# Pairs of score bursts, rows transposed in 32x32 blocks by VectorE, and a reordered hand-over from attention to experts

## The chip, the core and the metric

The kernel runs on one core of one Trainium2 chip. The metric is the device time of one execution in microseconds. Comparisons take the median over runs of both kernels on the same chip.

## What is computed

A gated cross-attention block followed by a gated mixture of experts, all in float32. `x` is 2048 x 256, the context 1601 x 256, there are 16 heads of 64, 8 experts of hidden size 512, and each row goes to its top 2 experts. The mask of the inputs keeps only rows at the end of the context: the kernel tests for that and then works on the last 401 context rows alone (a slower general branch exists and isn't taken).

```python
x = x + tanh(g_xattn) * xattn(layernorm(x), ctx, mask, Wq, Wk, Wv, Wo)
#   scores = q k^T / 8, masked, softmax over the context, times v, times Wo
x = x + tanh(g_ffn) * ffn(layernorm(x), Wg, W1, W2, W3)
#   gate_out = x Wg^T ; top 2 ; softmax of the two
#   per expert e: y = (silu(x W1[e]^T) * (x W2[e]^T)) W3[e]^T ; out += y * weight
```

## The kernel before

**Attention.** Heads go in pairs, rows in four groups of 512 (four tiles of 128). A *duo* is one tile of 128 rows for both heads of a pair; four duos (one group of rows, one pair of heads) are a *chunk*. There are 32 chunks and 128 duos. Every engine runs through the same list of steps n; each engine's `step_of(n)` says what it does in step n, and semaphores alone tie the engines together.

- TensorE (PE): step n has `scores(n)` (L1284): four products with 64 rows of weights, two heads beside one another in the array's halves, into two of the four banks `ps_s`. It is followed by one other piece: `queries` (L1227, `wq_sb`) where n % 4 is 1, `out_projection` (L1321, `wo_sb`) where it is 2, and the two halves of `probs_v` (L1311, the product with v, 64 columns of weights, two heads beside one another) where it is 3 and 0. `scores(d)` waits until VectorE has read duo d-2.
- VectorE (DVE): in step n the reciprocals of the sums of duo n-1 (`inverses`, L1029), scaling, mask and maximum of duo n (`mask_and_max`, L1040, PSUM to `probs`), and the 32x32 block transposes of duo n-2 (`transpose_blocks`, L1052) into `blocksT`.
- ScalarE (ACT): the exponentials of duo n (`exps`, L672), and copies out of PSUM.
- GpSimd (POOL): the division, i.e. the product of duo n-1 with its reciprocals (`scale`, L552).
- `regroup` (L331): when the four duos of chunk c are in `blocksT`, 16 DMAs per chunk (12 from SyncE's queue, 4 from ScalarE's) move the blocks to their partitions in `probsT`. `probs_v(c, 0)` waits for all of them, in step 4c + 11.
- Beside this, after each group of rows is finished, its routing runs in stages s (`routing(r, s)`, from step 47 + 32r on): norms, logits, the top two, positions. In stages 22 to 25 GpSimd scatters the rows of the group into `x_regrouped` in DRAM, sorted by expert: two indirect DMAs (L543) a stage, eight a group. The fourth group's routing runs beside the first expert tiles (`BESIDE`).

**Hand-over.** SyncE (SP) loads expert 0 (three DMAs of 512 KB, L277) between the regrouping of chunks 29 and 30. After the last regrouping has landed it loads expert 1, waits for the table of tiles (`sched_ready`, made by VectorE from step 133 on in pieces) and for the scatters of three groups, loads eight row tiles, and then the other experts.

**Experts.** 36 tiles of 128 rows go through: for tile s PE does `first_hidden(s+1)` (L1491), the transposes of `gated` (L1512), `second_hidden(s+1)` (L1491), `transpose_x` of tile s+2 (L1486: two transposes, copied out by ScalarE at L788) and `project_down(s)` (L1519). VectorE does `gate(s+1)` (L1172) and `weigh(s)`, GpSimd adds the rows to the output with an indirect DMA (L604). A row tile is one DMA of 128 rows of 258 words (`load_tile`, L384).

Of the kernel before, what the change touches and what calls it, by code (L numbers as in the profile page):

```python
# [13 lines left out]
P = 128  # L14
# [47 lines left out]
LAST_STAGE = 25  # L62

BESIDE = ((0, 1, 2, 3), (4, 5, 6, 7), (8, 9, 10), (12, 13, 14), (15, 16), (17, 18, 19, 20, 21), (22,), (23,), (24,), (25,))
# [3 lines left out]
K_STEPS = {0: 2, 6: 3, 7: 4, 8: 5, 10: 6, 12: 7}  # L68
XN_STEP = 20
# [9 lines left out]
def build(nc, x, ctxT, mask, g_xattn, g_ffn, Wq, Wk, Wv, Wo, WgT, W1T, W2T, W3T, out):  # L79
    with ExitStack() as ctx:  # L80
# [105 lines left out]
        with ExitStack() as ffn:  # L186

            w_sb = sb("w_sb", [P, NE, EW], F32, ffn)
            xgT = sb("xgT", [P, 2, KT, P], F32, ffn)
            silu = sb("silu", [P, FH], F32, ffn)  # L190
            to_blocks = sb("to_blocks", [P, 272], F32, ffn)
            xg = sb("xg", [P, RING, XW], F32, ffn)
# [58 lines left out]
        xgT_ps, xgT_ready = sem("xgT_ps"), sem("xgT_ready")  # L251
# [34 lines left out]

        def settled(eng):
# [19 lines left out]
            eng.wait_ge(inv_ready, PRE - 1)  # L307
            eng.wait_ge(scaled, PRE - 1)
            eng.wait_ge(blocks_ready, PRE - 2)
# [30 lines left out]
        def _(sp):  # L340
# [38 lines left out]
            def load_tile(i, k):  # L379
                s = RING * i + k  # L380
                if not first(s, RING):
                    sp.wait_ge(y_ready, s - RING + 2)
                row = table(sp, 0, s, NOWHERE)
                sp.dma_start(xg[:, k % RING, :], x_regrouped[bass.ds(row, P), :]).then_inc(xg_in[k % RING], 16)  # L384

            with sp.If(last_block_only(sp)):
                sp.wait_ge(pads_set, 2)
                for c in range(CHUNKS):
# [18 lines left out]
                for k in range(RING):  # L407
                    load_tile(0, k)
# [3 lines left out]
                load_expert(sp, 3)  # L412
# [48 lines left out]
            for s in range(FULL, NG):  # L461
                sp.wait_ge(xg_in[s % RING], 16 * (s // RING + 1))
# [5 lines left out]
        def _(pool):  # L468
# [33 lines left out]
            def routing(r, s):  # L502
# [37 lines left out]
                if 22 <= s < 22 + GT:  # L540
                    t = s - 22
                    for c in range(2):
# [4 lines left out]
            def scale(d):  # L547

                pool.wait_ge(inv_ready, d + 1)
# [5 lines left out]
            def step_of(n):  # L555
# [8 lines left out]
                if 1 <= n <= DUOS:  # L564
                    scale(n - 1)
# [59 lines left out]
        def _(act):  # L625
# [64 lines left out]
            def step_of(n):  # L690
# [20 lines left out]
                if n % 4 in (2, 3) and 0 <= (n - 6) // 4 < CHUNKS:  # L711

                    c = (n - 6) // 4
                    if n == 6:
# [4 lines left out]
                    for g in (0, 1) if n % 4 == 2 else (2, 3):  # L719
# [66 lines left out]
            def copy_xgT(s, buf):  # L786
                act.wait_ge(xgT_ps, s + 1)
                act.copy(xgT[:, buf, :, :], ps_t[1][:, 0:KT * P].rearrange("p (k n) -> p k n", k=KT))\  # L788
                   .then_inc(xgT_ready, 1)

# [12 lines left out]
            def ffn_tile(i, k):  # L803
# [4 lines left out]
                if not (isinstance(s, int) and s + 2 >= NG):  # L808
                    copy_xgT(s + 2, k % 2)

            act.sem_inc(gatedT_ready, 1)
            copy_xgT(0, 0)
            silu_of(0)
            copy_xgT(1, 1)
# [14 lines left out]
        def _(dve):  # L829
# [87 lines left out]
            def routing(r, s):  # L917
# [17 lines left out]
                if s in (6, 7):  # L935
# [8 lines left out]
                    for t in (2 * s - 12, 2 * s - 11):  # L944
                        dve.tensor_scalar(rows[:, 0, t, 0:D], xs[:, bass.ds(GT * r + t, 1), :].squeeze(1),
# [80 lines left out]
            def inverses(d):  # L1026
                b = 2 * d % RING_P
                dve.wait_ge(probs_ready, 2 * d + 2)
                dve.reciprocal(inv_sum[:, b:b + 2], sum_exp[:, b:b + 2]).then_inc(inv_ready, 1)  # L1029

            def mask_and_max(d):
# [3 lines left out]
                for u in (2 * d, 2 * d + 1):  # L1035
# [4 lines left out]
                    dve.tensor_tensor_reduce(probs[:, b, 0:LASTK], ps_s[u % 4][:, 0:LASTK], biases[:, tile, :],  # L1040
# [25 lines left out]
            def step_of(n):  # L1066
# [12 lines left out]
                if 1 <= n <= DUOS:  # L1079
# [514 lines left out]
```

## Time and profile before

| | |
|---|---|
| three runs, us | 657.89, 657.48, 655.51 (median 657.48) |
| the profiled execution, us | 657.01 |
| its span, first to last instruction | 655.3 us |
| PE busy | 622.2 us, 95% |
| DVE, POOL, ACT busy | 389.9, 308.2, 286.9 us |
| PE busy from 100 to 200 us | 100.00 of 100.00 us |
| PE busy from 394 to 430 us (hand-over) | 27.18 of 36.00 us |
| PE busy from 470 to 560 us (experts) | 90.00 of 90.00 us |
| granted TensorE clock, 400 to 403, 403 to 406, 406 to 409, 412 to 415, 415 to 418 us | 1.00, 0.53, 0.50, 0.76, 1.00 of 2.4 GHz |

The span is cut into three stretches: attention to about 396 us (the last scores), a hand-over to 428.7 us (the first product with an expert's weights), and the experts. 1.7 us of the execution lie outside the span.

### The profile page before, as it was taken

The numbers are of one execution on the slowest core, as the hardware profiler recorded it, in microseconds if no ns is written. First come the engines' busy times: TensorE is split into PE (matmuls) and PEld (weight loads), VectorE is DVE, ScalarE is ACT, GpSimd is POOL, SyncE is SP. The second block draws the span as 40 slices with busy tenths as digits, with TensorE's granted clock in tenths as the row PEclk, the third lists the DMA queues.
The fourth block names the chain that finished last, engine by engine and source line by source line (L and its number), as shares of the span: only waits on it lengthen the run. The fifth ranks groups of instructions, "written<-read, shape, count | busy, mean of one in ns | idle before, by whom it ended". The sixth has DMA issues, their size and how long they took to land.

```text
span 655.3 us, 10748 instructions
## 1 busy us (share of the span) xinstructions
PE 622.2 (95%) x2958; PEld 344.4 (53%) x2959; DVE 389.9 (59%) x1187; ACT 286.9 (44%) x744; POOL 308.2 (47%) x270
## 2 busy tenths in 40 slices
PE   4899999999999999999999997889999999999994
PEld 2444454545455554555544554346666666666653
DVE  3578968888988769978879977243252122221211
ACT  2765566565555545555546552023322222222221
POOL 3643645555564686564786545302463222222221
PEclk9999999999999999999999998899999999999999
DMA  8844675767667578566587769989455322233311
GB/s 320 291 106 106 135 161 124 167 147 164 152 135 185 133 189 184 136 159 162 144 202 147 174 161 239 257 280 355 74 144 124 48 44 47 41 48 48 48 21 22
DMA packets 93420, 95.37 MB, mean 146 GB/s; under 512 B 11312, under 2 KB 86960, under 8 KB 93360
## 3 DMA queue, kind: packets, MB, share of 16 engines
q1 hardware_dynamic: 70800, 71.64, 42.1%
q10 hardware_dynamic: 15840, 14.07, 9.5%
q0 software_dynamic: 6720, 8.95, 8.4%
q8 instruction: 27, 0.44, 0.3%
q14 instruction: 33, 0.27, 0.2%
HBM read 27.72 MB, written 12.36 MB: 61 GB/s over the span
## 4 chain that ended last, share of the span: by engine, by line
PE 76%; POOL 6%; DMA 5%; DVE 5%; issue 4%; ACT 3%; ACTq 1%; SPq 0%; POOLq 0%; DVEq 0%
PE ps_s L1491 17%; PE ps_s L1284 13%; PE ps_o L1311 13%; PE ps_o L1519 8%; PE ps_a L1227 7%; PE ps_a L1321 7%; POOL probs L552 3%; POOL x_regrouped L543 2%; DMA out_dram<-yg,ids 2%; PE ps_t L1512 2%; DVE blocksT L1052 2%; PE ps_o L1297 2%; DVE probs L1040 2%; DMA probsT<-blocksT 1%; PE ps_t L1486 1%
## 5 line engine op out<-in xcount | busy, mean ns | idle before, releaser
L552 POOL TENSOR_TENSOR probs<-probs,inv_sum 128x802 f32<-128x802 f32 x128 | 195.0, 1525 | 155.1 <-DVE inv_sum L1029 154.3
L672 ACT ACTIVATE probs<-probs,neg_max 128x401 f32<-128x401 f32 x256 | 159.3, 624 | 144.3 <-DVE neg_max L1040 144.3
L1040 DVE CUSTOM_DVE_ANT_0 probs<-ps_s,biases 128x401 f32<-128x401 f32 x256 | 136.9, 573 | 57.2 <-PE ps_s L1284 56.0
L1491 PE MATMUL ps_s<-w_sb,xgT 128*128 x296 | 139.5, 594 | 1.4 <-ACT xgT L788 1.4
L1052 DVE STREAM_TRANSPOSE blocksT<-probs 128x832 f32<-128x832 f32 x128 | 133.3, 1041 | 9.3 <-POOL probs L552 9.3
L604 POOL DMA_INDIRECT out_dram<-yg,ids x36 | 56.1, 1558 | 161.1 <-DVE yg L1184 142.9
L1311 PE MATMUL ps_o<-probsT,v_sb 128*64 128x512 f32 x512 | 125.8, 615 | 4.2 <-DMA probsT<-blocksT 4.2
L1284 PEld LDWEIGHTS ps_s<-kT,qT 64*128 64x128 f32 x1024 | 82.3, 186 | 78.0 <-DVE neg_max L1040 38.8
L1284 PE MATMUL ps_s<-kT,qT 64*128 64x201 f32 (+1 forms) x1024 | 121.2, 355 | 0.7 <-ACT qT L636 0.7
L1172 DVE TENSOR_TENSOR gated<-ps_s,silu 128x512 f32<-128x512 f32 x37 | 25.6, 692 | 118.5 <-PE ps_s L1491 113.1
L801 ACT COPY gatedT<-ps_t 128x512 f32<-128x512 f32 x36 | 21.1, 586 | 120.5 <-PE ps_t L1512 120.5
L1491 PEld LDWEIGHTS ps_s<-w_sb,xgT 128*128 128x128 f32 x296 | 53.0, 190 | 39.6 <-issue 38.0
L1519 PE MATMUL ps_o<-w_sb,gatedT 128*128 x288 | 68.1, 379 | 0.0
L1321 PE MATMUL ps_a<-wo_sb,oT 128*128 128x256 f32 x240 | 60.7, 397 | 4.0 <-ACT qT L636 3.7
L1227 PE MATMUL ps_a<-xnT,wq_sb 128*128 128x512 f32 x128 | 63.2, 616 | 0.8 <-ACT xnT L640 0.8
L1311 PEld LDWEIGHTS ps_o<-probsT,v_sb 128*64 128x64 f32 x512 | 31.8, 138 | 59.9 <-issue 54.6
L1519 PEld LDWEIGHTS ps_o<-w_sb,gatedT 128*128 128x128 f32 x288 | 51.9, 190 | 5.6
L1321 PEld LDWEIGHTS ps_a<-wo_sb,oT 128*128 128x128 f32 x240 | 43.7, 192 | 16.4 <-ACT qT L636 10.1
L672 ACT ACTIVATION_READ_ACCUMULATOR probs<-probs,neg_max 128x1 f32 x256 | 47.8, 187 | 0.0
L1184 DVE TENSOR_SCALAR yg<-ps_o,xg 128x256 f32<-128x256 f32 x36 | 17.4, 484 | 42.1 <-PE ps_o L1519 42.1
L543 POOL DMA_INDIRECT x_regrouped<-rows,place x32 | 31.7, 990 | 9.2 <-issue 8.3
L1227 PEld LDWEIGHTS ps_a<-xnT,wq_sb 128*128 128x128 f32 x128 | 21.8, 189 | 24.3 <-issue 24.3
(143 smaller groups left out, 418.0 us busy)
## 6 DMA issues: line engine op xcount, KB each, us to landing
probsT<-blocksT SPq DMA_DIRECT2D x285, 96.0 KB, 3.2
probsT<-blocksT SPq DMA_DIRECT2D x95, 128.0 KB, 2.6
probsT<-blocksT ACTq DMA_DIRECT2D x99, 96.0 KB, 3.2
xg<-x_regrouped SPq DMA_DIRECT2D x39, 129.0 KB, 2.1
probsT<-blocksT ACTq DMA_DIRECT2D x33, 128.0 KB, 2.7
w_sb<-W1T_dram SPq DMA_DIRECT2D x8, 512.0 KB, 7.8
w_sb<-W2T_dram SPq DMA_DIRECT2D x8, 512.0 KB, 8.5
w_sb<-W3T_dram SPq DMA_DIRECT2D x8, 512.0 KB, 9.4
```

Of the source, the lines that this page charges most:

```text
L543: pool.indirect_dma_start(out=x_regrouped, out_offset=bass.IndirectOffsetOnAxis(ap=place[:, c, t:t + 1], axis=0), in_=rows[:, c, t, :], in ...
L552: pool.tensor_tensor(duo, duo, inv_sum[:, u:u + 2].unsqueeze(2).to_broadcast([P, 2, LASTK]), ALU.mult)\
L604: pool.indirect_dma_start(out=out, out_offset=bass.IndirectOffsetOnAxis(ap=ids[:, k % RING:k % RING + 1], axis=0), in_=yg[:, k % 2, :], in ...
L672: act.activation(probs[:, b, 0:LASTK], probs[:, b, 0:LASTK], ACT.Exp, bias=neg_max[:, b:b + 1], scale=-1.0, accum_out=sum_exp[:, b:b + 1]) ...
L1040: dve.tensor_tensor_reduce(probs[:, b, 0:LASTK], ps_s[u % 4][:, 0:LASTK], biases[:, tile, :], HD ** -0.5, 3e38, ALU.add, ALU.min, neg_max[ ...
L1052: dve.transpose(blocksT[:, c % 2, :, :, t * 32:(t + 1) * 32].rearrange("p c u n -> p u c n"), probs[:, u:u + 2, :].rearrange("p u (c n) -> ...
L1227: mm = pe.matmul(ps_a[:, :], wq_sb[:, k, p * P:(p + 1) * P], xnT[:, k, i * GQ:(i + 1) * GQ], start=(k == 0), stop=(k == KT - 1))
L1284: mm = pe.matmul(ps_s[(2 * d + odd) % 4][:, k0:k1], qT[h0:h0 + HD, c % 2, t * P:(t + 1) * P], kT[h0:h0 + HD, c % HP, k0:k1], start=True, s ...
L1311: mm = pe.matmul(ps_o[odd * HD:(odd + 1) * HD, :], v_sb[:, s, 2 * (c % HP) + odd, :], probsT[:, c % 2, s, :, odd, :], start=(s == 0), stop ...
L1321: mm = pe.matmul(wo_bank(g, half)[:, n * D:(n + 1) * D], oT[:, c % 4, t * P:(t + 1) * P], wo_sb[:, c % HP, :], start=(c == 2 * g), stop=(c ...
L1491: mm = pe.matmul(bank[:, :], xgT[:, buf, k, :], w_sb[:, bass.ds(expert, 1), (n * KT + k) * FH:(n * KT + k + 1) * FH].squeeze(1), start=(k ...
L1519: mm = pe.matmul(ps_o[:, 0:D], gatedT[:, k, :], w_sb[:, bass.ds(expert, 1), 2 * KT * FH + k * D:2 * KT * FH + (k + 1) * D].squeeze(1), sta ...
```

## The change

1. **Bursts.** From duo 24 (`BURST`) on, PE does the scores of two duos in a row, in even steps, into six banks (the four `ps_s` and the two `ps_t`); a duo now waits for VectorE to have read the duo three before it.
2. **Two duos per reciprocal; everything behind it a step later.** VectorE inverts the sums of two duos in one instruction in even steps. `scale` is at step d + 2, `transpose_blocks` at step d + 3, ScalarE's share of the regrouping a step later. `probs_v` stays in its steps.
3. **Scatters.** One indirect DMA a stage over eight stages instead of two over four, for the first two groups; the third keeps two a stage. `BESIDE` keeps two a tile for the fourth.
4. **Block transposes of rows.** The row tile is loaded by five DMAs instead of one: four bring 64 of the 256 columns each, to 32 partitions, as pieces of 64 words (256 bytes); the fifth brings the two words of weight and row number. VectorE then makes `xgT` in one block transpose of 128 x 256, three tiles ahead. PE's `transpose_x` and ScalarE's copy are gone. The rows are stored with their columns in another order, and `WgT` is laid out to match.
5. **Hand-over.** SP loads no expert and stores no output rows while the last chunks are regrouped. After them: expert 0, the waits for table and scatters, tiles 0 and 1, the sign that expert 0 is there, expert 1, tile 2, the store of the third group, expert 2, and then for e = 3 to 7 tile e, expert e and the sign for expert e-1. VectorE makes the table of tiles in one go in step 133.

```diff
+BURST = 24
...
+        def scores_bank(u):
+
+            return ps_s[u % 4] if u < 2 * BURST else (ps_s + ps_t)[(u - 2 * BURST) % 6]
...
-                sp.dma_start(xg[:, k % RING, :], x_regrouped[bass.ds(row, P), :]).then_inc(xg_in[k % RING], 16)
+                tile = x_regrouped[bass.ds(row, P), :]
+                for q in range(4):
+
+                    sp.dma_start(xg_blocks[32 * q:32 * q + 32, k % RING, :, :],
+                                 tile[:, q * D // 4:(q + 1) * D // 4].rearrange("(b j) n -> j b n", j=32))\
+                      .then_inc(xg_in[k % RING], 16)
+                sp.dma_start(xw[:, k % RING, :], tile[:, D:]).then_inc(xg_in[k % RING], 16)
...
-                    if c in (13, 21, 29):
+                    if c in (13, 21):
                         store(c // 8 - 1)
-                    if c == CHUNKS - 3:
-
-                        sp.wait_ge(q_ready, CHUNKS)
-                        load_expert(sp, 0)
-                expert_there(0)
+
                 for slot in range(2):
                     sp.wait_ge(probsT_in[slot], 16 * REGROUP * CHUNKS // 2)
-                load_expert(sp, 1)
+                load_expert(sp, 0)
                 sp.wait_ge(sched_ready, 2)
                 sp.wait_ge(scattered, 16 * 2 * GT * (NR - 1))
-                for k in range(RING):
-                    load_tile(0, k)
+                load_tile(0, 0)
+                load_tile(0, 1)
+                expert_there(0)
+                load_expert(sp, 1)
+                load_tile(0, 2)
+                store(NR - 2)
 
                 sp.wait_ge(masked_ready, 2 * DUOS)
                 load_expert(sp, 2)
-                load_expert(sp, 3)
                 expert_there(1)
 
                 sp.wait_ge(pv_ready, CHUNKS)
-                for e in range(4, NE):
+                for e in range(3, NE):
+                    load_tile(0, e)
                     load_expert(sp, e)
-                    expert_there(e - 2)
-                expert_there(NE - 2)
+                    expert_there(e - 1)
                 expert_there(NE - 1)
...
+                each = 2 if isinstance(r, int) and r == NR - 2 else 1
+                for n in range(each * (s - 22), each * (s - 21)):
+                    if 0 <= n < 2 * GT:
+                        t, c = divmod(n, 2)
...
-                if 1 <= n <= DUOS:
-                    scale(n - 1)
+                if 2 <= n < DUOS + 2:
+                    scale(n - 2)
...
-                dve.wait_ge(probs_ready, 2 * d + 2)
-                dve.reciprocal(inv_sum[:, b:b + 2], sum_exp[:, b:b + 2]).then_inc(inv_ready, 1)
+                dve.wait_ge(probs_ready, 2 * d + 4)
+                dve.reciprocal(inv_sum[:, b:b + 4], sum_exp[:, b:b + 4]).then_inc(inv_ready, 1)
...
-                if 1 <= n <= DUOS:
-                    inverses(n - 1)
+                if n % 2 == 0 and 2 <= n <= DUOS:
+                    inverses(n - 2)
...
-                if 2 <= n < DUOS + 2:
-                    transpose_blocks(n - 2)
+                if 3 <= n < DUOS + 3:
+                    transpose_blocks(n - 3)
...
+            def transpose_x(i, k):
+
+                dve.wait_ge(xg_in[k % RING], 16 * 5 * (i + k // RING + 1))
+                dve.transpose(xgT[:, k % 4, :, :].rearrange("p h (b j) -> p b h j", j=32),
+                              xg_blocks[:, k % RING, :, :].rearrange("p b (h i) -> p b h i", i=32)).then_inc(xgT_ready, 1)
...
                 weigh(i, k)
+                if not (isinstance(s, int) and s + 3 >= NG):
+
+                    transpose_x(i, k + 3)
 
             dve.sem_inc(y_ready, 1)
+            for k in range(3):
+                transpose_x(0, k)
             gate(0)
...
-                if n < DUOS:
+                if n < BURST:
                     scores(n)
+                elif n % 2 == 0 and n < DUOS:
+                    scores(n)
+                    scores(n + 1)
...
-                if not (last and s + 2 >= NG):
-                    transpose_x(i, k + 2)
                 project_down(s, now)
```

On PE, four steps of attention behind duo 24, before (`ps_s` the scores, L1311 the product with v, L1227 the queries, L1321 the projection):

```order
L1311 MATMUL ps_o<-probsT,v_sb 64x512 x4
L1284 MATMUL ps_s<-kT,qT 128x201 x2
L1284 MATMUL ps_s<-kT,qT 128x200 x2
L1227 MATMUL ps_a<-xnT,wq_sb 128x512 x2
L1284 MATMUL ps_s<-kT,qT 128x201 x2
L1284 MATMUL ps_s<-kT,qT 128x200 x2
L1321 MATMUL ps_a<-wo_sb,oT 128x256 x4
```

and after, where the same lines have the numbers 1300, 1327, 1241 and 1337:

```order
L1300 MATMUL ps_s<-kT,qT 128x201 x2
L1300 MATMUL ps_s<-kT,qT 128x200 x2
L1300 MATMUL ps_t<-kT,qT 128x201 x2
L1300 MATMUL ps_t<-kT,qT 128x200 x2
L1327 MATMUL ps_o<-probsT,v_sb 64x512 x4
L1241 MATMUL ps_a<-xnT,wq_sb 128x512 x2
```

The scores of the second duo moved ahead of the product with v, which now stands directly before the queries.

On SP, the queue between the last regrouping and the experts, before:

```order
L331 DMA probsT<-blocksT 32x4x256 x2
L331 DMA probsT<-blocksT 32x3x256 x6
L277 DMA w_sb<-W1T_dram 128x2x512
L277 DMA w_sb<-W2T_dram 128x2x512
L277 DMA w_sb<-W3T_dram 128x4x256
L285 TENSOR_LOAD sched
L285 ISA x2
L384 ISA
L384 DMA xg<-x_regrouped 128x258
```

and after, where these weights are expert 0's and no longer expert 1's:

```order
L336 DMA probsT<-blocksT 32x4x256 x2
L336 DMA probsT<-blocksT 32x3x256 x6
L278 DMA w_sb<-W1T_dram 128x2x512
L278 DMA w_sb<-W2T_dram 128x2x512
L278 DMA w_sb<-W3T_dram 128x4x256
L286 TENSOR_LOAD sched
L286 ISA x2
L392 ISA
L392 DMA xg_blocks<-x_regrouped 32x4x64
L392 ISA
L392 DMA xg_blocks<-x_regrouped 32x4x64
```

Two more such DMAs and one of `128x2` complete the tile: one issue became five.

On VectorE, the first two expert tiles (before: no row of `xgT`), after:

```order
L1182 STREAM_TRANSPOSE xgT<-xg_blocks 128x4x2x32 x3
L1177 TENSOR_TENSOR gated<-ps_s,silu 128x512
...
L1189 CAST ids<-xw 128x1
L1193 TENSOR_SCALAR yg<-ps_o,xw 128x256
L1182 STREAM_TRANSPOSE xgT<-xg_blocks 128x4x2x32
```

The first product of the gate now stands behind the transposes of three tiles.

## Rows read from the trace of the kernel before

**Rows 1.** The page: busy us of each engine, share of the span, instructions.

```profile
PE 622.2 (95%) x2958; PEld 344.4 (53%) x2959; DVE 389.9 (59%) x1187; ACT 286.9 (44%) x744; POOL 308.2 (47%) x270
```

**Rows 2.** PE in order of time, attention: start, busy us, line, shape, count.

```profile
102.59 0.95 PE L1284 MATMUL ps_s<-kT,qT 64*128 64x201 f32 x8
103.47 1.99 PE L1321 MATMUL ps_a<-wo_sb,oT 128*128 128x256 f32 x8
105.39 0.95 PE L1284 MATMUL ps_s<-kT,qT 64*128 64x201 f32 x8
106.28 1.94 PE L1311 MATMUL ps_o<-probsT,v_sb 128*64 128x512 f32 x8
108.14 0.95 PE L1284 MATMUL ps_s<-kT,qT 64*128 64x201 f32 x8
```

**Rows 3.** The same view: two duos of scores together, transposes between pieces.

```profile
67.78 1.63 PE L1284 MATMUL ps_s<-kT,qT 64*128 64x201 f32 x16
69.34 1.94 PE L1311 MATMUL ps_o<-probsT,v_sb 128*64 128x512 f32 x8
...
84.15 1.09 PE L1238 MATMUL ps_t<-ident,xn_late 128*128 128x128 f32 x8
85.17 1.94 PE L1311 MATMUL ps_o<-probsT,v_sb 128*64 128x512 f32 x8
...
87.92 1.09 PE L1238 MATMUL ps_t<-ident,xn_late 128*128 128x128 f32 x8
88.85 1.88 PE L1227 MATMUL ps_a<-xnT,wq_sb 128*128 128x512 f32 x4
```

**Rows 4.** The view of waits (total, times, longest), and the longest on PE.

```profile
PE ps_a L1321 <- ACT qT L636: 3.7, 3, 1.5
...
253.56 1.99 PE L1321 MATMUL ps_a<-wo_sb,oT 128*128 128x256 f32 x8 [1.51 <-ACT qT L636]
```

**Rows 5.** POOL in order of time: two divisions with two scatters between them.

```profile
231.59 1.53 POOL L552 TENSOR_TENSOR probs<-probs,inv_sum 128x802 f32<-128x802 f32 x1
...
235.59 1.53 POOL L552 TENSOR_TENSOR probs<-probs,inv_sum 128x802 f32<-128x802 f32 x1
```

**Rows 6.** The page, DMA issues of the regrouping, and SP in order of time.

```profile
probsT<-blocksT SPq DMA_DIRECT2D x285, 96.0 KB, 3.2
...
381.81 8.69 SPq L331 DMA_DIRECT2D probsT<-blocksT  x12
```

**Rows 7.** The hand-over, in order of time: PE, POOL and SP.

```profile
404.04 0.30 POOL L525 TENSOR_SCALAR rows<-gap,tanh_g 128x4 f32<-128x4 f32 x1 [1.51 <-DVE gap L960]
...
408.38 6.15 PE L1311 MATMUL ps_o<-probsT,v_sb 128*64 128x512 f32 x16 [2.91 <-DMA probsT<-blocksT]
...
421.14 8.75 SPq L384 DMA_DIRECT2D xg<-x_regrouped  x8
...
428.67 3.69 PE L1491 MATMUL ps_s<-w_sb,xgT 128*128 x8 [0.66 <-ACT xgT L788]
...
435.15 0.60 PE L1512 MATMUL ps_t<-ident,gated 128*128 128x128 f32 x4
```

**Rows 8.** Row tiles and experts: SP issue ns, landing us; gate of tile 7.

```profile
L384 SPq DMA_DIRECT2D xg<-x_regrouped x39: 332/333/702, 421.1 to 619.1; - x39
...
xg<-x_regrouped SPq DMA_DIRECT2D x39, 129.0 KB, 2.1
...
w_sb<-W3T_dram SPq DMA_DIRECT2D x8, 512.0 KB, 9.4
...
476.26 0.69 DVE L1172 TENSOR_TENSOR gated<-ps_s,silu 128x512 f32<-128x512 f32 x1 [3.44 <-PE ps_s L1491]
```

**Rows 9.** One expert tile on PE, and the block transposes of attention (page).

```profile
505.10 0.38 PE L1486 MATMUL ps_t<-ident,xg 128*128 128x128 f32 x2
505.32 1.89 PE L1519 MATMUL ps_o<-w_sb,gatedT 128*128 x8
...
L1052 DVE STREAM_TRANSPOSE blocksT<-probs 128x832 f32<-128x832 f32 x128 | 133.3, 1041 | 9.3 <-POOL probs L552 9.3
```

More of the change, by code:

```diff
@@ L306, in settled @@
             eng.wait_ge(probs_ready, 2 * PRE)
[L307 to L309 removed]
+            eng.wait_ge(inv_ready, PRE // 2 - 1)
+            eng.wait_ge(scaled, PRE - 2)
+            eng.wait_ge(blocks_ready, PRE - 3)
         def wo_bank(g, half):
@@ L710, in step_of @@
                     mask_words(n + 1)
-                if n % 4 in (2, 3) and 0 <= (n - 6) // 4 < CHUNKS:
-                    c = (n - 6) // 4
-                    if n == 6:
+                if n % 4 in (3, 0) and 0 <= (n - 7) // 4 < CHUNKS:
+                    c = (n - 7) // 4
+                    if n == 7:
                         act.wait_ge(pads_set, 2)
@@ L718, in step_of @@
                         act.wait_ge(pv_ready, c - 1)
-                    for g in (0, 1) if n % 4 == 2 else (2, 3):
+                    for g in (0, 1) if n % 4 == 3 else (2, 3):
                         for b in (2, 3) if c == CHUNKS - 1 else (3,):
@@ L944, in routing @@
                     for t in (2 * s - 12, 2 * s - 11):
-                        dve.tensor_scalar(rows[:, 0, t, 0:D], xs[:, bass.ds(GT * r + t, 1), :].squeeze(1),
+                        row = rows[:, 0, t, 0:D].rearrange("p (q h i) -> p h q i", q=4, h=KT)
+                        dve.tensor_scalar(row, xs[:, bass.ds(GT * r + t, 1), :].squeeze(1).rearrange("p (h q i) -> p h q i", h=KT, q=4),
                                           r_mean_var[:, t, 0:1], var[:, 0, t:t + 1], ALU.subtract, ALU.mult)\
@@ L1039, in mask_and_max @@
                         dve.wait_ge(blocks_ready, (u - RING_P) // 2 + 1)
-                    dve.tensor_tensor_reduce(probs[:, b, 0:LASTK], ps_s[u % 4][:, 0:LASTK], biases[:, tile, :],
+                    dve.tensor_tensor_reduce(probs[:, b, 0:LASTK], scores_bank(u)[:, 0:LASTK], biases[:, tile, :],
                                              HD ** -0.5, 3e38, ALU.add, ALU.min, neg_max[:, b:b + 1])\
@@ L1097, in step_of @@
                     mask_flag()
-                if SCHED_STEP <= n < SCHED_STEP + 5:
-                    if n == SCHED_STEP:
-                        dve.wait_ge(routed, NR - 1)
-                    schedule(False, range(5 * (n - SCHED_STEP), min(5 * (n - SCHED_STEP) + 5, SCHED_OPS)))
+                if n == SCHED_STEP:
+                    dve.wait_ge(routed, NR - 1)
+                    schedule(False, range(SCHED_OPS))
             for n in range(PRE):
@@ L1477, in _ @@
                 full_attention()
-            def transpose_x(i, k):
-                s = RING * i + k
-                pe.wait_ge(xg_in[k % RING], 16 * (i + k // RING + 1))
-                if not (isinstance(s, int) and s == 0):
-                    pe.wait_ge(xgT_ready, s)
-                for c in range(KT):
-                    mm = pe.transpose(ps_t[1][:, c * P:(c + 1) * P], xg[:, k % RING, c * P:(c + 1) * P], ident[:, :])
-                mm.then_inc(xgT_ps, 1)
             def hidden(s, buf, expert, n, bank, done):
@@ L1534, in ffn_tile @@
                     ahead = table(pe, 1, s + 1, NE - 1)
-                    first_hidden(s + 1, (k + 1) % 2, ahead)
+                    first_hidden(s + 1, (k + 1) % 4, ahead)
                 transpose_gated(s)
                 if not (last and s + 1 >= NG):
-                    second_hidden(s + 1, (k + 1) % 2, ahead)
+                    second_hidden(s + 1, (k + 1) % 4, ahead)
                 now = table(pe, 1, s, NE - 1)
-                if not (last and s + 2 >= NG):
-                    transpose_x(i, k + 2)
                 project_down(s, now)
@@ L1578 @@
         "Wo": a["L0_xattn_Wo"],
-        "WgT": a["L0_ffn_Wg"].T,
+        "WgT": a["L0_ffn_Wg"].T.reshape(2, 4, 32, 8).transpose(1, 0, 2, 3).reshape(256, 8),
         "W1T": a["L0_ffn_W1"].transpose(0, 2, 1),
```

42 lines of the change are left out of this document (15 added, 27 removed).

## The prediction

> **What bounds the kernel now.** I read the shares of the page first [rows 1]: PE is busy 95% of the span, every other engine under 60%. So time is won on PE, or in the few places where PE waits. Then PE in order of time, and from start to start, since each row's busy time overlaps the next. In attention [rows 2] a step is a burst of scores (102.59 to 103.47, 0.88 us) and one other piece (projection 1.92 us, product with v 1.86 us); queries take 1.91 us. A chunk is 4 x 0.88 + 1.91 + 1.92 + 2 x 1.87 = 11.09 us without a gap. In the experts [rows 9] it is the same: no gap, and the two transposes of rows take 505.10 to 505.32, 0.22 us. PE stands still only in two stretches: briefly after the scatters [rows 4], and in the hand-over [rows 7], where at 408.38 it waits 2.91 us for the regrouping and then runs 16 products in 6.15 us that take two times 1.86 us in [rows 2] (the lower clock level). The first product of the experts is at 428.67.
>
> **Part 1, bursts.** What does a change of array form cost? Two duos of scores in a row take 1.56 us (67.78 to 69.34, [rows 3]), two single ones 1.76: a pair saves 0.20. The other piece gains too only if its neighbour has its own form. Transposes in full form take 1.02 us before a product with v but 0.93 before queries [rows 3], so each border between forms costs about 0.1 on either side, and the border between the product with v and a full-form piece is one of them. Before, four duos have eight borders; in bursts (scores, scores, v, queries, scores, scores, projection, v) they have six. That is 0.40 us per chunk: 11.09 becomes 10.69. Steps 24 to 123 are 50 pairs: 50 x 0.20 = 10.0 us. The routing matmuls of three groups, which now lie beside full-form pieces, lose two borders each: 3 x 2 x 0.2 = 1.2 us.
>
> The Trainium skill, TensorEngine Tiling (Array Packing), section Key Properties, says that changing the tiling mode drains TensorE, while changing the tile doesn't. The rows agree, and they put a price of 0.2 us on it; the page gives none.
>
> **Part 2, scatters.** A division takes 1.53 us, and one followed by two scatters 4.00 us from start to start [rows 5], more than PE's step of 2.77; so GpSimd falls behind, and the chain reaches PE twice: of the 3.7 us in three waits [rows 4] two (1.51 and the next one after the second group) are this. With one scatter a step it is 1.53 + 1.24 = 2.77 us a step against PE's new 2.67, for eight steps: 0.8 us behind, which the ring of four duos covers. I count 2.8 us won; if the cover fails, none.
>
> **Part 3, everything a step later.** Reciprocals fall from 128 to 64, all on VectorE, which isn't the bound: nothing. But the last transposes of a chunk stand in step 4c + 6 and the product with v still in 4c + 11. VectorE finishes them about 2.9 us after the burst of 4c + 6 starts (scores 0.8, mask 1.0, transposes 1.04). Twelve issues take 8.1 to 8.7 us from first to last and land 3.2 us later [rows 6]: 13.5 to 14.8 us. PE is there two pairs (10.69) + 1.56 + 1.92 = 14.2 us after that burst. Before, with the transposes one step of 2.77 us earlier, there were about 3 us to spare; now there is about nothing, and in routing steps VectorE has up to 0.9 us more a step. A wait moves all the following bursts too, so it refills its own cover. Bounds: 0, and 0.3 us for each of 26 chunks, 8 us. I take 2, since most chunks have no routing. Attention then reaches its last four duos 10.0 + 1.2 + 2.8 - 2.0 = 12.0 us earlier.
>
> **Part 4, hand-over.** The chain to the experts goes: last scores, VectorE, division, transposes, third group's routing on GpSimd (404.04), scatters, table, first tile load (421.14, [rows 7]). It keeps its steps, but at its start there is one more block transpose to catch up with (1.04, [rows 9]) and the two last divisions follow one reciprocal, one after the other (1.53 more, less what overlaps): 2.1 us longer. So the first tile load is at 421.14 - 12.0 + 2.1 = 411.2. The 9 us that the regrouping waited behind expert 0's weights are no longer on this chain; the drain is shorter, but the scatters end last, so by themselves the quieter drain and the lower clock there are worth nothing. Now SP issues more: eight tile loads took 8.75 us, 1.09 each, of which the DMA itself 0.33 [rows 8]. Five DMAs, four of them like regrouping ones (0.65 with the gap), are 0.76 + 4 x 0.65 + 0.33 = 3.7 us a tile. The sign for expert 0 comes after two tiles: 411.2 + 7.5 = 418.7. Before the first gate VectorE wants tile 2: behind expert 1's issues (1.6 us) and its own (3.7), landing 2.1 us later [rows 8] or a little more beside the weights, with transposes and gate (1.0): 427.4, against 435.15 before for the transposes of `gated` that wait for it. PE would be there at 424; the wait is 3.4 us. If the clock falls in that pause, this same wait covers it.
>
> **Part 5, experts.** Each tile loses 0.22 us on PE. VectorE gains one block transpose of 256 columns, about 256 / 832 x 1041 = 320 ns, in a tile of 5.8 us in which it is busy under 2: hidden. From 435.15 to the gate of tile 7 at 476.26 it was 41.1 us; now 41.1 - 7 x 0.22 = 39.6, so it is due at 467.0. But it needs tile 8 in blocks, which SP loads only after all experts: from 418.7 on seven experts (7 x 1.6), six tiles (6 x 3.7), a store (0.6), about 1 us of waiting for each sign (6) and the landing of the last expert (5.5; 9.4 in [rows 8] is with several under way) give 464.5, and tile 8 with its landing and transposes 470.7. So 3.7 us more are lost. From there the span ran 655.3 - 476.26 = 179.0 us; 28 row transposes less, 172.9.
>
> **The sum.** 470.7 + 172.9 = 643.6 us of span, and 1.7 us outside it: **645.3 us** against the profiled execution's 657.01 (the median is 657.48). Since that gate is bound by the loads, what attention saves passes through to the end, and most of what the early experts save does not.
>
> **The rivals.**
> - *Nothing starves*: the landing of the regrouping stays within its cover (+2.0), the signs come without waiting and expert 7 lands early (+3.7), and the drain loses nothing (+2.1). 645.3 - 7.8 = 637.5 us. For it: the issue times of the regrouping are upper values. Against it: expert 7's sign stands before tile 8 whatever happens.
> - *The product with v waits in every chunk* (part 3's upper bound): 6 us more, 651.3, and with the upper bound of landing in the start of the experts 654.
> - *Small pieces crowd the queues.* A tile is 512 pieces of 256 bytes and 128 of 8 bytes instead of 128 of 1032, while the weights fill the DMA engines. If a piece costs as much as a larger one, a tile takes five times the queue time, and each of six tiles delays its expert by about 1.5 us: 645.3 + 9 = 654. The Trainium skill, DMA: Bandwidth & Descriptors, section Specifications, wants at least 512 bytes for full rate, and speaks against this part of the change; no row before shows a load in 256-byte pieces.
> - *The experts become bound by SP's queue*, and the kernel slower. PE's tile is 5.6 us; at 3.7 us SP has room. The issue of the new DMAs is the unknown: if each took 1.2 us instead of 0.65 (a weights issue rises over 1 us when queues are full), a tile would cost 0.76 + 4 x 1.25 + 0.4 = 6.2 us, and 33 tiles 0.6 us each, 20 us, so 665 us. It decides above 1.05 us a DMA. Against it: the DMA engines are mostly idle there, and a tile is prefetched from far ahead.
>
> **How the numbers follow.** Forecast 0.55; nothing starves 0.15; the product with v waits 0.13; small pieces 0.10; SP bound 0.07. About 0.5% (3.3 us) is what a measurement of this kernel can tell from none. Below 653.7 lie the forecast, the first rival and most of the second, and part of the third: faster 0.84; from 653.7 to 660.3 the rest of these: same 0.09; slower 0.07. The range goes from below the first rival to the upper bounds of the second and third, 635 to 654.
>
> **What would show it.** Bursts: x16 rows of scores starting every 5.34 us in attention, and a chunk of 10.7. Part 2: no wait of 1.5 us after scatters. Part 3: waits of the product with v for DMAs; over 4 us in all before the last four duos and 2.0 is too low. Part 4: the first tile load near 411, the first expert product near 419, then a pause of PE of about 3 us before the first transposes of `gated`. Part 5: SP's pitch of 3.7 us a tile, a pause before the gate of tile 7, and then a tile of 5.60 us. A tile pitch on SP over 5.6 us, or a late chunk in every pair, would make the forecast wrong.

## The result and the profile after

The changed kernel takes 661.03 us (median of 5 runs, 660.22 to 663.02); the kernel before, on the same chip, 657.48 us. The ratio is 1.0057, with an interval of 1.0029 to 1.0085: slightly slower, where 645.3 us was forecast. The profiled execution has a span of 658.5 us, against 643.6 in the sum.

The page's busy line, as [rows 1]:

```profile
PE 609.7 (93%) x2882; PEld 342.9 (52%) x2883; DVE 415.6 (63%) x1162; ACT 272.1 (41%) x706; POOL 306.4 (47%) x270
```

PE's view of waits (total us, times, longest), as [rows 4]:

```profile
PE ps_a L1337 <- ACT qT L648: 8.4, 4, 2.3
...
PE ps_o L1327 <- DMA probsT<-blocksT: 3.4, 4, 1.8
PE ps_a L1241 <- ACT rowsT L668: 3.3, 3, 1.1
```

PE is busy 12.5 us less (about 19 were planned: 11.2 in attention and 0.22 for each of 35 tiles), and the span is 3.2 us longer. VectorE has 64 reciprocals fewer and 39 small transposes more (17.0 us), and yet it is busy 25.7 us longer: at least 8.7 us that no added instruction accounts for. And PE waits 8.4 us for `qT` instead of 3.7.

The bursts themselves are there. PE in order of time, as [rows 2] and [rows 3]:

```profile
99.88 1.63 PE L1300 MATMUL ps_s<-kT,qT 64*128 64x201 f32 x16
105.22 0.95 PE L1300 MATMUL ps_t<-kT,qT 64*128 64x201 f32 x8
...
110.58 0.95 PE L1300 MATMUL ps_s<-kT,qT 64*128 64x201 f32 x8
```

A pair starts every 5.35 us, a chunk takes 10.70; 5.34 and 10.69 were forecast. Still, the burst of the last four duos starts at 393.99, where the kernel before starts duo 124 at 388.99: 5.0 us later, not 12.0 earlier. From there on the milestones keep close to the forecast. The hand-over in order of time, SP and PE, as [rows 7]:

```profile
421.76 0.39 SPq L278 DMA_DIRECT2D w_sb<-W1T_dram  x1
...
430.37 1.91 SPq L392 DMA_DIRECT2D xg_blocks<-x_regrouped  x4
...
434.38 1.81 SPq L392 DMA_DIRECT2D xg_blocks<-x_regrouped  x4
...
436.94 8.31 PE L1501 MATMUL ps_s<-w_sb,xgT 128*128 x12 [3.62 <-SPq L382]
445.61 0.65 PE L1522 MATMUL ps_t<-ident,gated 128*128 128x128 f32 x4 [0.35 <-DVE gated L1177]
```

The pause of about 3 us before the first transposes of `gated` is only 0.35 us: the 12 products before it took 8.31 us, where four take 1.72 us from start to start behind it (446.10 to 447.82). The granted clock was 0.50 from 437 to 441 us and 0.77 from 441 to 445.

**Where the time went.** By milestones against the forecast: the last four duos 17.0 us late; from there to the first tile load 36.4 us (2.1 more than forecast); from the load to the first transposes of `gated` 15.2 (1.0 less); from these to the end 212.9 (3.3 less). Together 14.9 = 658.5 - 643.6. So the miss lies in attention, at a few places. From 60 us to its last four duos PE stands idle 17.2 us, against 3.7 before. The longest wait for `qT` (2.27 us, ending at 79.85) also costs clock: the granted clock was 1.00 up to 81 us and 0.50 from 81 to 84. VectorE by line and form between 30 and 420 us (busy us, mean ns), first of before, then of after:

```profile
L945 DVE TENSOR_SCALAR rows<-xs,r_mean_var,var 128x256 f32<-128x256 f32 x12 | 4.2, 391 | 0.0
L907 DVE TENSOR_TENSOR won<-won,rank 128x32 f32<-128x32 f32 x6 | 1.0, 172 | 0.1
L835 DVE TENSOR_SCALAR var<-r_mean_var 128x4 f32<-128x4 f32 x3 | 0.4, 128 | 0.0
```

```profile
L950 DVE TENSOR_SCALAR rows<-xs,r_mean_var,var 128x256 f32<-128x256 f32 x12 | 7.2, 644 | 0.0
L910 DVE TENSOR_TENSOR won<-won,rank 128x32 f32<-128x32 f32 x6 | 4.4, 735 | 0.1
L838 DVE TENSOR_SCALAR var<-r_mean_var 128x4 f32<-128x4 f32 x3 | 3.6, 1204 | 0.0
```

The instructions are the same; some now last nine times as long. With L865 and L842, which grow as well (from 4.2 to 7.1 and from 1.3 to 4.7 us), it is 15.9 us. What stands beside them shows in the order of time, DVE and POOL of after:

```profile
170.81 0.18 DVE L1035 RECIPROCAL inv_sum<-sum_exp 128x4 f32<-128x4 f32 x1
171.07 3.00 POOL L564 TENSOR_TENSOR probs<-probs,inv_sum 128x802 f32<-128x802 f32 x2 [1.96 <-DVE inv_sum L1035]
171.93 1.04 DVE L1058 STREAM_TRANSPOSE blocksT<-probs 128x832 f32<-128x832 f32 x1
172.89 1.20 DVE L838 TENSOR_SCALAR var<-r_mean_var 128x4 f32<-128x4 f32 x1
174.13 0.17 DVE L840 TENSOR_SCALAR var<-var 128x4 int32<-128x4 int32 x1
```

One reciprocal for two duos releases two divisions in a row, 171.07 to 174.07. The transpose beside them keeps its 1.04 us. The TENSOR_SCALAR of four columns behind it ends at 174.09, with the second division. The next masks stand behind it on VectorE, ScalarE's exponentials wait for these, and the copies of `qT` stand behind the exponentials; there PE waits. In the kernel before, one division of 1.53 us [rows 5] is over before masks (1.1 us) and transposes (1.04 us) are, so the small instructions at the end of a step never met it.

The Trainium skill, SBUF — State Buffer, section Who interferes with whom, says that VectorE and GpSimd share one pair of ports as an exclusive lock: an instruction of VectorE with two inputs in SBUF, or a copy or `tensor_scalar` in a two-port mode, fully blocks until the GpSimd instruction that started first is over (with two inputs, only if that one reads SBUF). The trace agrees to 0.02 us (174.09 against 174.07); the mode that the TENSOR_SCALAR ran in no row shows. I had not weighed this rule.

### The profile page after: what moved, and what is told of

It is laid out like the page before. It is cut to its first block, busy times and chain, and to the rows that moved or that the text cites. A ratio compares the mean times of both kernels' runs of the same rounds, so it can differ in the third digit from the quotient of the medians.

```text
span 658.5 us, 10943 instructions
## 1 busy us (share of the span) xinstructions
PE 609.7 (93%) x2882; PEld 342.9 (52%) x2883; DVE 415.6 (63%) x1162; ACT 272.1 (41%) x706; POOL 306.4 (47%) x270
## 2 busy tenths in 40 slices
DMA packets 115886, 95.39 MB, mean 145 GB/s; under 512 B 38768, under 2 KB 109424, under 8 KB 115824
## 4 chain that ended last, share of the span: by engine, by line
PE 57%; DVE 17%; issue 7%; DMA 6%; ACT 4%; SPq 4%; POOL 4%; ACTq 2%; POOLq 0%; DVEq 0%
PE ps_s L1501 17%; PE ps_o L1529 8%; PE ps_o L1327 7%; DVE blocksT L1058 6%; PE ps_s L1300 6%; PE ps_a L1241 5%; DVE probs L1046 5%; PE ps_a L1337 4%; DMA out_dram<-yg,ids 2%; SPq L336 2%; PE ps_t L1522 2%; ACT probs L684 2%; POOL probs L564 2%; PE ps_t L1300 2%; PE ps_o L1313 2%
## 5 line engine op out<-in xcount | busy, mean ns | idle before, releaser
L564 POOL TENSOR_TENSOR probs<-probs,inv_sum 128x802 f32<-128x802 f32 x128 | 192.6, 1523 | 162.0 <-DVE inv_sum L1035 161.2
L1501 PE MATMUL ps_s<-w_sb,xgT 128*128 x296 | 142.3, 605 | 3.7 <-SPq L382 3.6
L1046 DVE CUSTOM_DVE_ANT_0 probs<-ps_s,biases 128x401 f32<-128x401 f32 x188 | 100.3, 571 | 37.9 <-PE ps_s L1300 35.1
L1300 PEld LDWEIGHTS ps_s<-kT,qT 64*128 64x128 f32 x752 | 62.6, 187 | 41.0 <-issue 31.9
L1300 PE MATMUL ps_s<-kT,qT 64*128 64x201 f32 (+1 forms) x752 | 83.2, 348 | 0.7 <-ACT qT L648 0.7
L1337 PE MATMUL ps_a<-wo_sb,oT 128*128 128x256 f32 x240 | 62.2, 404 | 9.9 <-ACT qT L648 8.4
L1529 PEld LDWEIGHTS ps_o<-w_sb,gatedT 128*128 128x128 f32 x288 | 54.7, 190 | 22.8 <-issue 17.2
L1046 DVE CUSTOM_DVE_ANT_0 probs<-ps_t,biases 128x401 f32<-128x401 f32 x68 | 36.3, 572 | 8.9 <-PE ps_t L1300 7.7
L1193 DVE TENSOR_SCALAR yg<-ps_o,xw 128x256 f32<-128x256 f32 x36 | 17.4, 483 | 31.8 <-PE ps_o L1529 30.8
```

What stands on the lines that cost most here:

```text
L564: pool.tensor_tensor(duo, duo, inv_sum[:, u:u + 2].unsqueeze(2).to_broadcast([P, 2, LASTK]), ALU.mult)\
L1046: dve.tensor_tensor_reduce(probs[:, b, 0:LASTK], scores_bank(u)[:, 0:LASTK], biases[:, tile, :], HD ** -0.5, 3e38, ALU.add, ALU.min, neg_m ...
L1300: mm = pe.matmul(scores_bank(2 * d + odd)[:, k0:k1], qT[h0:h0 + HD, c % 2, t * P:(t + 1) * P], kT[h0:h0 + HD, c % HP, k0:k1], start=True, ...
L1337: mm = pe.matmul(wo_bank(g, half)[:, n * D:(n + 1) * D], oT[:, c % 4, t * P:(t + 1) * P], wo_sb[:, c % HP, :], start=(c == 2 * g), stop=(c ...
L1501: mm = pe.matmul(bank[:, :], xgT[:, buf, k, :], w_sb[:, bass.ds(expert, 1), (n * KT + k) * FH:(n * KT + k + 1) * FH].squeeze(1), start=(k ...
L1529: mm = pe.matmul(ps_o[:, 0:D], gatedT[:, k, :], w_sb[:, bass.ds(expert, 1), 2 * KT * FH + k * D:2 * KT * FH + (k + 1) * D].squeeze(1), sta ...
```

## The experiments

Theory A: the two divisions in a row reach into the end of VectorE's step and hold its small instructions. Rivals: the bursts themselves, which let the queries and the routing share bank `ps_a` more tightly (B), and the lateness of a reciprocal that waits for two duos (C). Times are medians; the kernel before took 656.17, 657.55 and 657.69 us beside the three sets of four.

**One reciprocal and one division a step.**

```diff
-                if n % 2 == 0 and 2 <= n <= DUOS:
-                    inverses(n - 2)
+                if 1 <= n <= DUOS:
+                    inverses(n - 1)
...
-                if 2 <= n < DUOS + 2:
-                    scale(n - 2)
+                if 1 <= n <= DUOS:
+                    scale(n - 1)
...
```

> The changed kernel with one part undone: reciprocals of one duo per instruction and the division one step after its duo, as before (block transposes stay a step later, bursts stay). Theory A: two divisions in a row (3.00 us on GpSimd) hold something that VectorE's instructions with two SBUF operands or plain SBUF copies need, so VectorE's small instructions wait up to 1.3 us each, and through ScalarE PE waits for qT. Then the mean of the normalise rows of the late groups (633 ns), of the routing's var product (434 ns) and won product (594 ns) fall back to about 391, 151 and 175 ns, the waits of 2.27 us near 79 us and 2.15, 2.20, 1.78 us before the third projection of each routing shrink below 1 us each, and the last scores (397.4 us) come 8 to 11 us earlier: ratio to before about 0.99. Theory B (the bursts alone cost it, by taking the scores from between routing and queries): the waits stay, less than 2 us won, ratio 1.00 to 1.006.

Measured: 646.88 us, ratio 0.9858 (0.9840 to 0.9877). The last four duos start at 381.19, 12.8 us earlier than in the changed kernel. By line and form, DVE, as above, and then PE's waits:

```profile
L950 DVE TENSOR_SCALAR rows<-xs,r_mean_var,var 128x256 f32<-128x256 f32 x12 | 4.2, 388 | 0.0
L838 DVE TENSOR_SCALAR var<-r_mean_var 128x4 f32<-128x4 f32 x3 | 0.4, 128 | 0.0
```

```profile
PE ps_o L1327 <- DMA probsT<-blocksT: 4.3, 7, 2.5
PE ps_a L1241 <- ACT rowsT L668: 2.4, 3, 0.9
...
PE ps_a L1337 <- ACT qT L648: 0.4, 1, 0.4
```

The lengths are back, and PE's 8.4 us of waits for `qT` became 0.4. 14.2 us come back from an edit that adds 64 instructions.

**No bursts.** In the changed kernel `BURST = DUOS`.

> The changed kernel without bursts (scores of one duo in every step, four banks); everything else as in the change. Theory A: VectorE's long small instructions stay; the 10 us of array switches are lost again and so is what the bursts cost at the routing's bank (about 2 us a group, 6 in all): 3 to 8 us slower than the change. Theory B: the stalls of 4.8 us a group vanish, 14 us, for 10 us of switches: about 4 us faster than the change.

Measured: 663.44 us, ratio 1.0105 (1.0077 to 1.0132). The long instructions stay (632 ns for L865), so the bursts are not their cause.

**Bursts apart where routing reads `ps_a`.**

```diff
-                if n < BURST:
-                    scores(n)
-                elif n % 2 == 0 and n < DUOS:
-                    scores(n)
-                    scores(n + 1)
+                alone = n < BURST or group_of(n - n % 2)[1] in (9, 17)
+                if n < DUOS and (alone or n % 2 == 0):
+                    scores(n)
+                    if not alone:
+                        scores(n + 1)
```

> The changed kernel, but the two pairs of duos of each routing in which routing products are followed by the queries on the same bank (stages 9 and 17) are taken apart again, so that scores stand between them. Theory B in its exact form: the waits of 1.10 us (queries for rowsT) and 0.86 us (queries for counts) go, three times, at the price of 0.2 to 0.4 us of switches each: 3.5 to 5 us faster than the change. The waits for qT (2.15, 2.20, 1.78) and for the residual (0.67) stay. Theory A alone: no change.

Measured: 660.58 us, ratio 1.0068 (1.0049 to 1.0087); not to be told from the changed kernel. But the edit hardly touched the waits that it was made for (for `rowsT` and `counts` 5.0 us in the changed kernel, 4.0 here), so it alone says little against B. What clears the bursts is the run without them, which was slower and not faster, and the paced run below, which keeps them.

**Both, single reciprocals and bursts apart.**

> Both e1's and e3's edits. If A and B are two separate costs, their gains add: 12 to 16 us faster than the change, ratio to before 0.982 to 0.988. If they are one cost (VectorE late either way), it is no faster than the better of the two.

Measured: 644.91 us, ratio 0.9825 (0.9804 to 0.9846): 2.0 us under the first experiment, with the last scores 1.2 us earlier, and 16.1 us under the changed kernel, where the two edits won 14.2 and 0.4 us by themselves. The bank probably costs a little once the collision is gone; the waits for `rowsT` fall only from 2.4 to 1.8 us.

**Paired reciprocals, divisions paced.** This and the next tell A from C, since in the first experiment both pairings went at once.

```diff
             def scale(d):
                 pool.wait_ge(inv_ready, d // 2 + 1)
+                if d % 2:
+                    pool.wait_ge(masked_ready, min(2 * d + 5, 2 * DUOS))
```

> The changed kernel with one edit on GpSimd: the second division of a pair waits until the first mask of the next step has run, so that GpSimd's divisions lie one to a step again, as in the kernel before. The reciprocals stay paired, the transposes at n - 3, the bursts stay. Theory A (two divisions in a row, 3.00 us, reach into the end of VectorE's step, where the small instructions of routing stand; these then stand still until the second division ends): VectorE's instructions fall back to their old lengths (L865 391 ns, L838 about 140, L842 about 150, where the changed kernel has 633, 946 and 434), PE's waits for qT fall from 8.4 us to under 1, and the time is 645 to 649 us. Rival C (it is the pairing of the reciprocals itself: they wait for the exponentials of a duo more, and all behind them comes late): the lengths may fall, but the time stays at 656 to 661 us.

Measured: 646.98 us, ratio 0.9865 (0.9825 to 0.9905). POOL and DVE in order of time (from here on L1037 is the reciprocal, L840 the TENSOR_SCALAR that was L838):

```profile
167.32 0.18 DVE L1037 RECIPROCAL inv_sum<-sum_exp 128x4 f32<-128x4 f32 x1
167.58 1.52 POOL L566 TENSOR_TENSOR probs<-probs,inv_sum 128x802 f32<-128x802 f32 x1 [0.34 <-DVE inv_sum L1037]
169.40 0.13 DVE L840 TENSOR_SCALAR var<-r_mean_var 128x4 f32<-128x4 f32 x1
171.42 1.52 POOL L566 TENSOR_TENSOR probs<-probs,inv_sum 128x802 f32<-128x802 f32 x1 [2.32 <-DVE neg_max L1048]
```

PE's view of waits of this kernel:

```profile
PE ps_a L1339 <- ACT qT L650: 0.9, 3, 0.5
```

One added wait on the engine that is not the bound, and 14.0 us come back with the reciprocals still paired. The last four duos start at 380.31, 13.7 us earlier than in the changed kernel: from 60 us on PE is idle 5.3 us instead of 17.2 and busy 1.8 us less.

**Single reciprocals, divisions in a row.** GpSimd waits for the second reciprocal, then divides both duos:

```diff
-                if 2 <= n < DUOS + 2:
+                if n % 2 == 0 and 2 <= n <= DUOS:
+                    pool.wait_ge(inv_ready, n)
                     scale(n - 2)
+                    scale(n - 1)
...
```

> The changed kernel with single reciprocals, one a step at n - 1 as before, but with GpSimd's two divisions of a pair still in a row: it waits for the second of the two reciprocals and then divides both. Theory A: VectorE's small instructions stay stretched (L865 about 630 ns, L838 about 900) and the time is 656 to 662 us, though no reciprocal waits for a pair. Rival C: 645 to 649 us, as with single reciprocals and single divisions (646.88 us measured).

Measured: 662.43 us, ratio 1.0084 (1.0055 to 1.0113). The same two views:

```profile
171.84 3.00 POOL L564 TENSOR_TENSOR probs<-probs,inv_sum 128x802 f32<-128x802 f32 x2 [2.02 <-DVE inv_sum L1037]
173.67 1.19 DVE L840 TENSOR_SCALAR var<-r_mean_var 128x4 f32<-128x4 f32 x1
```

173.67 + 1.19 = 174.86, with the divisions' end at 174.84. Rival C is refuted from both sides: pairing the reciprocals costs nothing, running the divisions in a row costs it all.

**Routing right behind the reciprocal.** On top of the first experiment, `routing(r, s)` stands ahead of `mask_and_max(n)` in VectorE's step. No division is paired (line numbers are again those of the changed kernel).

> The kernel of the first experiment (single reciprocals, single divisions, 646.88 us), but VectorE's routing instructions stand ahead of the masks of their step, right behind the reciprocal that starts GpSimd's 1.52 us division, instead of behind masks and transpose. Theory A: the first TENSOR_SCALAR or TENSOR_TENSOR of such a step stands still until the division ends (1.2 to 1.5 us instead of 0.13 to 0.39), masks come as much later, and the time is 655 to 670 us though GpSimd never has two divisions in a row. Rival: an instruction of four columns beside one division costs nothing, as most of those of before: the only loss is the order itself, 0.3 to 0.8 us a step at which TensorE has a duo in hand, and the time is 646 to 650 us.

Measured: 682.35 us, ratio 1.0382 (1.0355 to 1.0409): 35.5 us lost, more than either expected. DVE and POOL in order of time:

```profile
168.92 0.15 DVE L838 TENSOR_SCALAR var<-r_mean_var 128x4 f32<-128x4 f32 x1
169.08 1.52 POOL L564 TENSOR_TENSOR probs<-probs,inv_sum 128x802 f32<-128x802 f32 x1 [0.99 <-DVE inv_sum L1035]
169.10 1.52 DVE L840 TENSOR_SCALAR var<-var 128x4 int32<-128x4 int32 x1
...
177.52 1.52 POOL L564 TENSOR_TENSOR probs<-probs,inv_sum 128x802 f32<-128x802 f32 x1 [2.79 <-DVE inv_sum L1035]
177.53 1.52 DVE L844 SCALAR_TENSOR_TENSOR var<-var 128x4 f32<-128x4 f32 x1
...
189.23 1.52 POOL L564 TENSOR_TENSOR probs<-probs,inv_sum 128x802 f32<-128x802 f32 x1 [2.28 <-DVE inv_sum L1035]
189.40 0.75 DVE L1065 SCALAR_TENSOR_TENSOR xs<-ps_a,tanh_g,xs 128x512 f32<-128x512 f32 x1 [0.25 <-PE ps_a L1337]
```

An instruction of four columns lasts until the division that it meets is over. The one whose first input is in PSUM (`ps_a`) keeps its 0.75 us beside a division. With the same 1226 instructions VectorE is busy 437.2 us, against 404.6 in the first experiment, 32.6 us longer for the same work. The order moves the masks too, by the length of the routing instructions; how much of the 35.5 us is that was not separated.

**Single reciprocals, no bursts.**

> Single reciprocals and single divisions as in the first experiment (646.88 us), and the bursts taken away (scores of one duo per step to the end). What the bursts are worth where nothing else holds the step: the prediction's 10 us + 1.2 us of borders would give 656 to 658 us; in the changed kernel itself taking them away cost only 2.4 us (661.03 to 663.44). If bursts are worth only that little anywhere, 649 to 650 us.

Measured: 651.97 us, ratio 0.9920 (0.9895 to 0.9945). The bursts are worth 5.1 us, so the time lies between the two expectations.

**Single reciprocals, transposes a step earlier** (`transpose_blocks(n - 2)`, and the regrouping DMAs with them).

> Single reciprocals as in the first experiment (646.88 us), and the block transposes and the regrouping DMAs a step earlier, as in the kernel before (n - 2). The step later was put at +2 us in the prediction through PE's waits for probsT; the first experiment's trace shows 4.3 us of these waits. If these are owed to the step, the time is 643 to 645 us; if a transpose that stands right behind its division stops VectorE in the bursts, it is above 647 us.

Measured: 643.66 us, ratio 0.9801 (0.9775 to 0.9827), 3.2 us under the first experiment. PE's waits for `probsT` go from 4.3 us to 2.9, all of it in one wait in the drain (behind the last scores). This is the base of the next three.

**Expert 0's weights at the third chunk from the end**, as before the change.

> The kernel of the experiment with single reciprocals and the transposes a step earlier (643.66 us), and expert 0's three weight loads issued at the third chunk from the end, as in the kernel before, in place of behind the drain. In the base the last context product ends at 413.6 and TensorE waits 7.33 us for SyncE's word that expert 0 is there; the scatters' last issue ends at 408.7 but the tile loads start at 414.6, behind these weights. If the drain without other loads is a loss in itself, the scatters land by about 411, the first tile is loaded from 411.3 and the first expert product starts at 416 to 417: 639 to 641 us. Rival: the 1.5 MB of weights stand before the last regroups, TensorE waits up to 4 us more for probsT, and the time is 642 to 645 us.

Measured: 641.80 us, ratio 0.9757 (0.9731 to 0.9782). SP and PE in order of time, first of the base, then of this kernel:

```profile
405.49 3.65 PE L1327 MATMUL ps_o<-probsT,v_sb 128*64 128x512 f32 x16 [2.86 <-DMA probsT<-blocksT]
...
414.63 2.07 SPq L392 DMA_DIRECT2D xg_blocks<-x_regrouped  x4
...
420.94 6.96 PE L1501 MATMUL ps_s<-w_sb,xgT 128*128 x12 [7.33 <-SPq L382]
```

```profile
405.25 6.63 PE L1329 MATMUL ps_o<-probsT,v_sb 128*64 128x512 f32 x16 [4.48 <-DMA probsT<-blocksT]
...
410.01 1.92 SPq L392 DMA_DIRECT2D xg_blocks<-x_regrouped  x4
...
422.84 8.13 PE L1503 MATMUL ps_s<-w_sb,xgT 128*128 x12 [6.49 <-DVE xgT L1184]
```

The tile load comes 4.6 us earlier, as the theory had it, but the product with v waits longer and the first expert product starts later. That execution took 644.82 us. The median is 1.9 us under the base with intervals that overlap: the sign is likely, not shown.

**Expert 0's weights right behind the last regroup.**

> Same base (643.66 us); expert 0's weights are issued behind the last regroup, without waiting until the regroups have landed (some 5 us earlier than in the base, at about 400 in its trace). The regroups stand ahead of them in SyncE's queue. Theory: the weights are there at about 411 and the scatters land at 411 to 412, so that the first expert product starts 3 to 4 us earlier: 639.5 to 641.5 us. Rival: the last regroups and the scatters share the rings with the weights and land later by what was gained: 642.5 to 644.5 us.

Measured: 643.47 us, ratio 0.9796 (0.9769 to 0.9823), the same as the base. What the earlier weights win, PE's wait for `probsT` takes back (5.6 us against 2.9, and 4.7 before the first expert product against 7.3).

**Two scatters a step again.** `each = 2` for all groups.

> Same base (643.66 us), but the scatters of groups 0 and 1 two in a step again (with the division 4.0 us of GpSimd in a step of 2.67), as in the kernel before. The prediction's part 2 puts one scatter a step at 2.8 us, so 646 to 647 us. Rival: with the bursts in place the steps are long enough in pairs and PE has two duos in hand: within 0.5 us, 643.2 to 644.2 us.

Measured: 650.21 us, ratio 0.9885 (0.9857 to 0.9914): 6.6 us lost. PE waits for `qT` 5.5 us in 4 times, against 0.9 in the base. The step is 4.0 us on GpSimd again (divisions at 229.60 and 233.58).

## Why the prediction was wrong

**The step that failed** is the sentence in part 3, "Reciprocals fall from 128 to 64, all on VectorE, which isn't the bound: nothing". I costed the reciprocals and not what they release. Two divisions in a row keep GpSimd busy 3.00 us, and VectorE's small instructions wait for the second. Pacing the divisions and nothing else gives 646.98 us, single reciprocals and divisions 646.88, and with single reciprocals two divisions in a row give 662.43 again. It costs 14 us, nearly the whole distance from 645.3 to 661.03, and 11.5 us without bursts (663.44 against 651.97). None of the rivals named it: all looked at DMAs. Part 4 did see two divisions follow one reciprocal, but only as 1.53 us more of GpSimd's own work at the hand-over.

**That the repaired kernel meets the forecast is partly luck.** Its last four duos are at 381.19, 4.2 us later than forecast, and the experts give most of that back.

- *Part 1 (-11.2).* The mechanism held: 10.70 us a chunk. In the first experiment 20 plain duos, queries to queries, take 53.47 us (100.41 to 153.88), without bursts 55.47 (99.89 to 155.36): 0.10 us a duo, as costed. But at the last four duos only 5.5 us are left (386.69 to 381.19): from 60 us to there PE is busy 8.7 us less with bursts (315.7 against 324.3) and idle 3.2 us more (5.5 against 2.4). At the entry 0.5 is lost (100.41 against 99.89). And in routing PE's pieces now run into their producers: between 183 and 275 us PE waits 1.7 us (for `rowsT`, `counts` and `probsT`) with bursts and 0.4 without, and the same again between 275 and 367. The 1.2 us of borders did not show.
- *Part 2 (-2.8).* Too small. With bursts in place the scatters one a step are worth 6.4 us at the last four duos (386.55 to 380.12), 4.6 us of them PE's waits for `qT`. Parts 1 to 3 together, 7.8 us in the first experiment (388.99 to 381.19), were put at 12.0.
- *Part 3, the step later (+2).* 3.2 us by the run with the earlier transposes, but only 1.1 us of them at the last four duos (381.19 to 380.12), where the 2 had been put. The mechanism was right: six waits for `probsT` before the drain, 1.8 us, are gone. Its lower bound was added up wrongly: 2.9 + 8.1 + 3.2 us is 14.2, not 13.5.
- *Part 4.* The chain to the first tile load grew by 4.2 us (36.4 against 32.15), not 2.1. The last scatter is issued by 424.85, the load comes 5.5 us later; before, 3.6 (417.57 to 421.14). Expert 0's weights, issued from 421.76, lie between. In the kernel with early weights it is 2.6 us (407.44 to 410.01). No row shows the 9 us that the regrouping was said to wait behind expert 0's weights: with the weights ahead of it PE's wait in the drain is 4.48 us, without them 2.86. A tile takes SP 3.0 to 4.1 us (3.7 forecast), its four block DMAs mostly 1.8 to 1.9 (2.6 forecast), and the first transposes of `gated` followed the load after 15.2 us (16.2).
- *Part 5.* 0.22 us for each of 33 tiles is 7.3 us; from the first transposes of `gated` to the end it is 220.1 before and 212.9 after, 7.2. The 3.7 us that I added for tile 8 shrank to 0.3: the transposes of `gated` on PE start at 483.24 and 489.18, 5.94 us apart instead of 5.60. DVE in order of time:

```profile
480.80 0.69 DVE L1177 TENSOR_TENSOR gated<-ps_s,silu 128x512 f32<-128x512 f32 x1 [4.70 <-ACT silu L802]
486.58 0.45 DVE L1182 STREAM_TRANSPOSE xgT<-xg_blocks 128x256 f32<-128x256 f32 x1 [4.37 <-DMA xw<-x_regrouped]
486.95 0.65 DVE L1177 TENSOR_TENSOR gated<-ps_s,silu 128x512 f32<-128x512 f32 x1
```

The gate of tile 7 does stand behind the transposes of tile 8, which wait 4.37 us for their DMA, but a tile is 5.6 us, so it is only 6.15 us behind the gate of tile 6. The sum also took this gate for a place on PE's path. In the kernel before, the transposes that read it start 3.4 us later (479.67 against 476.26), so a late gate has slack that the sum left out. A small transpose takes 437 ns (320 forecast), hidden.

**Rivals.** SP as the bound did not happen: the experts ran at 5.6 us a tile. Small pieces, neither: there are 38768 packets under 512 bytes (11312 before), but a block load of 32 KB lands 2.1 us after its issue, as a whole tile of 129 KB did [rows 8], and tiles keep their 5.60 us. The Trainium skill, DMA: Bandwidth & Descriptors, section Specifications, wants 512 bytes for full rate. At one tile in 5.6 us the smaller pieces held nothing up; what they cost at full load no run shows. The product with v waited 3.4 us in all in the changed kernel, where PE was late itself, and 4.3 in the first experiment.

## What to carry to other kernels

An instruction that costs nothing where it stands can decide when another engine starts and how long it runs without a gap. For each wait that an edit merges, write down the merged run of the other engine (here 2 x 1.5 us) beside the time until the first instruction that it can block (2.1 us). If two engines can hold each other up in SBUF, as VectorE and GpSimd did here, look at mean durations by form first: the same line with another mean points to a collision, and one wait that paces the long instruction may repair it, as 14 us for one line did here.

## What the runs showed that I had not expected

- A TENSOR_SCALAR or SCALAR_TENSOR_TENSOR of four columns in SBUF lasts until GpSimd's TENSOR_TENSOR beside it is over (1.52 us instead of 0.16), and the view of waits does not name it: the time is in the busy time of the blocked instruction. Block transposes and masks out of PSUM keep their lengths.
- GpSimd waits too, by what is left of VectorE's instruction: a division that began under a running TENSOR_SCALAR took 1.61 us instead of 1.52, in the kernel with routing first. In both cases the later one waits.
